# Weights of eight experts split into bf16 pairs in DRAM, and a quantised FFN whose work is shared out anew

## The chip, the cores and the metric

The kernel runs on one core of a Trainium2 chip. The metric is the device time of one execution in microseconds, and the lower it is the better. TensorE (PE) does matrix products and transposes, VectorE (DVE) and ScalarE (ACT) work on rows in SBUF and PSUM, GpSimd (POOL) does small work and issues gathers, scatters and casting DMAs, and SyncE (SP) issues the other DMAs.

## The reference, cut to what matters

The input x has 16 sequences of 128 tokens with 256 features; ctx_1024 has the same shape. Two layers follow one another, each an attention over the context and then a feed-forward network (FFN), with a layer norm before each and a residual sum after it.

```python
# layer 0: attention, 16 heads, softmax over the context's tokens of the same sequence
x = x + softmax(q @ k.T * scale) @ v @ Wout
# layer 0: FFN whose activations and weights are rounded to 8-bit levels
def _act_fake_quant(x, clip_factor):
    scale = jax.nn.sigmoid(clip_factor) * jnp.max(jnp.abs(x)) / QMAX
    return jnp.clip(_ste_round(x / scale), -QMAX - 1.0, QMAX) * scale
h = _act_fake_quant(jax.nn.silu(gate) * up, clip_down[0])     # 704 hidden columns
x = x + einsum(h, _weight_fake_quant(w_down))
# layer 1: mLSTM attention, 4 heads, gates from q, k and v of all tokens
# layer 1: mixture of 8 experts, each token goes to its 2 best
#   expert e: (silu(x @ w1[e]) * (x @ w3[e])) @ w2[e], w1, w3: 256 x 1024, w2: 1024 x 256
```

The maximum in the scale of an activation runs over all tokens and columns, so the FFN of layer 0 has two places where everything has to be finished before anything goes on.

## The kernel before, in words

All engines run their own program and meet at semaphores. The stages follow one another.

**Attention of layer 0.** A step per sequence b, 16 in all. PE writes scores of two groups of heads (`scores`), DVE subtracts the row maximum (`softmax_shift`), ACT takes the exponential and copies, PE transposes and multiplies. POOL's only part is `mask_k(b, p)`: two products of 256 columns that lay out k by heads, after ACT's copy `qk_evac` and before `scores(b)` of the next step. SP loads the context of sequence b + 2 when `t1_done` says that b's is used. In the last seven steps DVE also does a piece of the weight quantisation of layer 0's FFN (`rest`: `gate_up_maxima` to `early_norms`), long passes over weights in SBUF. At the very start POOL does four powers for the norms and then its first mask.

**Quantised FFN.** `activation_scale(0)`: DVE takes a maximum per partition, POOL one over partitions (`partition_all_reduce`). Then four groups g of 512 tokens with six column tiles t: PE does gate and up (`gate_up`), ACT the Silu (`silu`), DVE the product with the scales and a maximum over its result (`hidden`). After `activation_scale(1)` eight half groups n pass through the down product: DVE clips in two passes (`clip_above`, `clip_below`), ACT stores as bf16, PE multiplies, DVE scales the result, adds it to x and takes the statistics of the next norm (`add_down`). `x2_ready` counts the half groups that are added.

**Attention of layer 1.** PE does transposes, gates and scores of all sequences (`front_c`, `gates_and_scores`); SP loads the contexts for it. When `gates_read` says that all are done, SP stores the gates to DRAM and loads them back in another order (L419, L422), DVE scans them, SP stores and broadcasts the running maxima, POOL masks (`causal`), and then the sequences pass through the values and the router.

**Routing and experts.** DVE works out which token goes to which of 39 tiles of 128 rows (`NT` = 39); a tile belongs to one expert. A tile passes through `gate_up_half` twice, transposes and `down_d` on PE. Each product is made of three bf16 products: x and the weights are split into a high half and a low one (what the high half leaves). Tokens are gathered for a tile by POOL (`gather_rows`), results are added to `sum_dram` by a scattering DMA (`add_rows`). The weights of an expert come from the inputs as float32 when its first tile is near: SP loads w1, w3 and w2 under the condition `new > 0` into `stage` (`load_part`), ACT writes the high half (`weights_high`), DVE or POOL subtracts for the low one (`weights_low`), and PE waits for `part_low` at each tile. There are three places for experts in SBUF (`SLOTS`).

```python
            for t in range(2):
                for n in range(3):
                    load_part(n, t, t)
```

Of the kernel before, what the change touches and what calls it, by code (L numbers as in the profile page):

```python
# [8 lines left out]
def build(nc, x, ctx_in, wq, wkv, wout, clip_x, clip_down, w_gate, w_up, w_down, ig_k, ig_b, fg_k, fg_b, rms_scale,  # L9
# [10 lines left out]
    P = 128  # L20
# [17 lines left out]
    SLOT = 2 * 3 * PART  # L38
    H1 = ig_k.shape[1]
# [12 lines left out]
    with stack:  # L52
# [9 lines left out]
        def lay(region, *specs):  # L62
# [59 lines left out]
        tile_info = sb("tile_info", [P, 3, NT], I32)  # L122
# [9 lines left out]
        down_out = sb("down_out", [P, 2, D])  # L132
# [25 lines left out]

        hT, x1n, xq = lay(region2, (F32, IT, B * P), (F32, B, D), (BF16, KT, B * P))
# [18 lines left out]
         hT_hi, hT_lo, y_d, w_col, stage) = lay(  # L178
# [6 lines left out]
            (F32, 2, 3, PART))  # L185

        xrow, xn_r, xT_r, logits = lay(region2[:, 2 * SLOT // 2:], (F32, B, ROW), (F32, 2, D), (F32, 2, KT, P), (F32, B, E))
        expert_w = region2[:, :].bitcast(BF16)
        xrow_dram = nc.dram_tensor("xrow_dram", (B * P + P, ROW), F32, kind="Internal").ap()
# [72 lines left out]
        amax_all_ready = sem("amax_all_ready")  # L262
# [6 lines left out]
        amax_h_step = sem("amax_h_step")  # L269
        h_clipped = sem("h_clipped")  # L270
# [51 lines left out]
        tokens_placed = sem("tokens_placed")  # L322
# [8 lines left out]
        gap_ready = sem("gap_ready")  # L331
# [3 lines left out]
        places_done = sem("places_done")  # L335
# [3 lines left out]
        part_loaded = [[sem(f"part_loaded{i}_{p}") for p in range(2)] for i in range(3)]  # L339
        part_high = [sem(f"part_high{i}") for i in range(3)]  # L340
        part_low = [sem(f"part_low{i}") for i in range(3)]
# [30 lines left out]
        def _(sp):  # L372
# [9 lines left out]

            whole = (IT - 1) * P
# [18 lines left out]
            with sp.Fori(0, B // 2 - 1) as i:  # L402
                for p in range(2):

                    sp.wait_ge(t1_done, 2 * i + p + 1)
                    sp.dma_start(ctx_sb[:, p, :], ctx_in[2 * i + (p + 2), :, :]).then_inc(ctx_loaded[p], 16)
# [4 lines left out]
            with sp.Fori(0, B // 2 - 1) as i:  # L411
                for p in range(2):

                    sp.wait_ge(ct_done, 2 * i + p + 1)
                    sp.dma_start(ctx_c[:, p, :], ctx_in[2 * i + (p + 2), :, :]).then_inc(cctx_loaded[p], 16)
# [22 lines left out]
            with sp.Fori(0, B // 2 - 1) as i:  # L438
                for p in range(2):
                    sp.wait_ge(pvc_done, 2 * i + p + 1)  # L440
                    load_v(p, 2 * i + (p + 2))
# [9 lines left out]
            def load_part(n, t, p, inner=False):  # L451
# [3 lines left out]
                if inner or t >= 2:  # L455

                    sp.wait_ge(part_low[n], t - 1)
# [5 lines left out]
            for t in range(2):  # L463
                for n in range(3):
                    load_part(n, t, t)
# [1384 lines left out]
```

## Time and profile before

| | us |
|---|---|
| median of three runs (range) | 881.13 (877.24 to 881.49) |
| the profiled execution: its own time | 880.42 |
| the profiled execution: span from the first to the last instruction | 878.7 |
| PE, DVE, ACT, POOL busy in the span | 686.7, 545.8, 394.6, 248.4 |
| mean granted TensorE clock, of full speed | 0.867 |

Durations are taken from the profiled execution. Its time lies 1.7 us above its span, and 0.7 us under the median of the three runs. A mean over the span says little here, since the stages have different limits.

### The profile page before, as it was taken

How to read it: one execution, taken by the hardware profiler on the slowest of the kernel's cores; microseconds unless marked ns; L12 is line 12 of the kernel's file. 1: busy time of each engine (PE TensorE's matmuls, PEld its weight loads, DVE VectorE, ACT ScalarE, POOL GpSimd, SP SyncE). 2: the span in 40 equal slices, each digit the busy share in tenths (PEclk: the TensorE clock that was granted, in tenths of full speed). 3: DMA queues.
4: the chain of work that ended last, by engine and by line, in shares of the span. 5: the costliest groups of instructions: out<-in, count | busy, mean ns of one | idle time of the engine just before them, and what ended most of it. 6: DMA issues, size and time to landing. Idle time of an engine off the chain costs nothing.

```text
span 878.7 us, 19300 instructions
## 1 busy us (share of the span) xinstructions
PE 686.7 (78%) x4567; PEld 473.8 (54%) x4611; DVE 545.8 (62%) x1394; ACT 394.6 (45%) x811; POOL 248.4 (28%) x372
## 2 busy tenths in 40 slices
PE   3999999983745695277616989898989989889992
PEld 2778877761223473266513556565655655556661
DVE  5577789974989654398785464555455455564440
ACT  1466655544633254355314453535444545453330
POOL 3111111110000200644402353545344272653421
PEclk9799999985985598555556999999999999999996
DMA  8100000000000111511172433343251515431113
GB/s 256 31 13 14 15 12 12 0 1 0 1 0 0 31 54 30 211 31 30 41 248 66 127 73 87 104 125 73 37 160 24 167 30 166 127 72 24 30 25 108
DMA packets 45843, 58.41 MB, mean 66 GB/s; under 512 B 13496, under 2 KB 39416, under 8 KB 45272
## 3 DMA queue, kind: packets, MB, share of 16 engines
q1 hardware_dynamic: 38328, 47.79, 16.7%
q0 software_dynamic: 7488, 10.31, 7.4%
q8 instruction: 11, 0.18, 0.1%
q14 instruction: 16, 0.13, 0.0%
HBM read 145.90 MB, written 11.80 MB: 179 GB/s over the span
## 4 chain that ended last, share of the span: by engine, by line
PE 47%; DVE 20%; issue 15%; POOL 7%; DMA 3%; ACT 3%; DVEq 2%; ACTq 1%; POOLq 1%; SPq 0%
PE psum L962 16%; PE psum L984 7%; PE psum L698 3%; PE psum L975 3%; PE psum L682 3%; PE psum L705 2%; POOL region L638 2%; PE psum L862 2%; DVE region L1455 2%; PE psum L718 1%; PE psum L737 1%; DMA region<-xrow_dram,next_token 1%; PE psum L687 1%; PE psum L855 1%; POOL region L561 1%
## 5 line engine op out<-in xcount | busy, mean ns | idle before, releaser
L962 PE MATMUL psum<-region 128*128 x897 | 209.3, 381 | 18.9 <-issue 6.0
L962 PEld LDWEIGHTS psum<-region 128*128 128x128 bf16 x936 | 91.7, 98 | 117.8 <-issue 28.6
L984 PE MATMUL psum<-region 128*128 x936 | 113.9, 280 | 6.3 <-DVE region L1799 3.7
L984 PEld LDWEIGHTS psum<-region 128*128 128x128 bf16 x936 | 92.1, 100 | 23.1 <-issue 9.7
L1769 DVE TENSOR_TENSOR region<-psum,region 128x512 f32<-128x512 f32 x78 | 53.9, 691 | 72.8 <-ACT region L1209 63.5
L1209 ACT ACTIVATE region<-psum 128x512 f32<-128x512 f32 x78 | 46.5, 597 | 116.6 <-PE psum L962 108.2
L620 POOL DMA_INDIRECT sum_dram<-region,tok_idx x39 | 62.0, 1589 | 6.9 <-issue 6.6
L608 POOL TENSOR_TENSOR pause_p<-minus_half 128x1 f32<-128x1 f32 x37 | 7.1, 193 | 192.3 <-DVE next_token L1785 191.6
L1230 ACT ACTIVATE pause_a<-one_col 128x1 f32<-128x1 f32 x117 | 23.7, 202 | 83.9 <-issue 68.8
L1799 DVE TENSOR_TENSOR region<-psum,region 128x1024 bf16<-128x1024 f32 x39 | 47.7, 1222 | 19.1 <-ACT region L1217 19.1
L522 POOL TENSOR_TENSOR region<-region,pair_mask 128x256 f32<-128x256 f32 x32 | 18.9, 613 | 138.3 <-ACT region L1029 138.3
L609 POOL DMA_INDIRECT region<-xrow_dram,next_token x39 | 41.0, 1052 | 39.6 <-DVE next_token L1764 27.4
L1749 DVE MEMSET pause_d<- 128x1 f32 x80 | 4.7, 59 | 73.4 <-ACT pause_a L1233 39.1
L1304 DVE TENSOR_REDUCE region<-psum 128x8 f32<-128x1024 f32 x32 | 39.0, 1219 | 14.6 <-PE psum L698 14.5
L1217 ACT ACTIVATE region<-psum 128x1024 bf16<-128x1024 f32 x39 | 39.9, 1023 | 16.0 <-PE psum L975 15.0
L1232 ACT ACTIVATE region<-region 128x2048 f32 x24 | 45.8, 1909 | 0.0
L895 PE MATMUL psum<-region 128*128 128x96 f32 x128 | 32.0, 433 | 17.6 <-DVE region L1579 8.8
L1033 ACT ACTIVATE region<-region 128x1024 f32<-128x1024 f32 x32 | 33.8, 1057 | 25.8 <-DVE region L1306 25.8
L1751 DVE TENSOR_TENSOR region<-region 128x2048 f32 x17 | 39.0, 2294 | 2.6 <-issue 2.6
L698 PE MATMUL psum<-region 32*128 32x256 f32 x256 | 38.1, 417 | 3.0 <-POOL region L522 3.0
L975 PEld LDWEIGHTS psum<-ident,region 128*128 128x128 f32 x312 | 36.5, 141 | 7.4
L975 PE MATMUL psum<-ident,region 128*128 128x128 f32 x312 | 40.4, 273 | 0.0
(295 smaller groups left out, 1362.6 us busy)
## 6 DMA issues: line engine op xcount, KB each, us to landing
region<-in_L_ffn_w SPq DMA_DIRECT2D x117, 1024.0 KB
region<-in_ctx SPq DMA_DIRECT2D x48, 128.0 KB, 2.1
region<-neg_max_dram SPq DMA_DIRECT2D x4, 1024.0 KB, 7.6
xrow_dram<-region SPq DMA_DIRECT2D x1, 2080.0 KB, 7.8
x_sb<-in_x SPq DMA_DIRECT2D x4, 512.0 KB, 6.6
sum_dram<-x_sb SPq DMA_DIRECT2D x1, 2048.0 KB, 7.5
region<-in_L_ffn_w_down SPq DMA_DIRECT2D x1, 704.0 KB, 8.3
region<-in_L_ffn_w_gate SPq DMA_DIRECT2D x1, 640.0 KB, 8.9
```

Source lines behind the costliest of these rows:

```text
L609: pool.indirect_dma_start(xg[:, p, :], None, xrow_dram, bass.IndirectOffsetOnAxis(ap=next_token[:, p:p + 1], axis=0)).then_inc(xg_loaded[p ...
L620: pool.indirect_dma_start(sum_dram, bass.IndirectOffsetOnAxis(ap=tok_idx[:, p:p + 1], axis=0), y_d[:, p, :], None, compute_op=ALU.add).the ...
L698: last = mm(S_ps[s][:, 4 * r + 2 * m:4 * r + 2 * m + 2, :], qkT[rows, p, m, :], kbd[rows, p, m, :, :], start=True, stop=True)
L962: last = mm(psum[:, 2 * f + n, :], (xT_lo if xl else xT_hi)[:, p, k, :], weights_at(place, wl, n, k * F1 + f * FH, FH), start=(i == 0), st ...
L975: last = tr(bank(4, F1 // P, P, count=2)[:, f, :], h_d[:, p, f * P:(f + 1) * P], ident[:])
L984: last = mm(psum[:, 7, 0:D], (hT_lo if hl else hT_hi)[:, f, :], weights_at(place, wl, 2, f * D, D), start=(i == 0), stop=(i == 3 * (F1 // ...
L1209: act_fn(sil_d[:, f, :], psum[:, 2 * f, :], ACT.Silu).then_inc(sil_d_ready, 1)
L1217: act_fn(hT_hi, bank(4, F1 // P, P, count=2), ACT.Copy).then_inc(hT_high, 1)
L1232: act_fn(expert_w[:, bass.ds(place + n * PART, PART)], stage[:, p, n, :], ACT.Copy)
L1304: nc.vector.tensor_reduce(row_max[:, m, :], S_ps[m][:, :, :], AX.X, ALU.max).then_inc(max_ready, 1)
L1769: tt(h_d[:, p, f * FH:(f + 1) * FH], psum[:, 2 * f + 1, :], sil_d[:, f, :], ALU.mult).then_inc(h_d_ready, 1)
L1799: tt(hT_lo, bank(4, F1 // P, P, count=2), hT_hi, ALU.subtract).then_inc(hT_low, 1)
```

## The change: what it does

**Weights.** Each of the 24 parts (8 experts, w1, w3 and w2, 1 MB of float32 each) is split once and lies then in DRAM as `split_dram`, a high and a low half of bf16 side by side. For a part, SP loads the float32 weights, a casting DMA that POOL issues loads the same weights as bf16, POOL subtracts in four chunks of 512 columns, and SP stores the pair (1 MB). The first 16 parts go beside the 16 steps of layer 0's attention, with three buffers; the other 8 after `x2_ready`, beside the first half of layer 1's attention, with two buffers. The first two experts are loaded as pairs into their places during the values of layer 1's attention. In the expert stage SP loads the others in the order of their use, by registers from `expert_info`; PE waits for `expert_loaded` by a count that stands in `tile_info`; ACT, DVE and POOL convert nothing there. The context loads of layer 1's first half are issued by ACT.

**Quantised FFN.** The maximum over partitions comes from a product of a matrix of ones with a diagonal (`spread_peak`) in place of POOL's reduction. Of the column tiles with odd t, ACT also copies the scaled up product out of PSUM and POOL makes the product with the Silu; DVE keeps the maxima and the even tiles. In the down stage ACT scales and rounds, DVE clips once, POOL does the residual sum. A Silu of one column loads the activation table early. In `token_stats` the copy of the statistics becomes a maximum over one element.

```diff
+            def load_part(i):
+                view, width = weight_part(i)
+                if i >= 2:
+                    sp.wait_ge(part_split, i - 1)
+                sp.dma_start(whole_part(i)[0].rearrange("p (t f) -> p t f", f=width), view).then_inc(part_loaded[ring_of(i)], 16)
+            def store_part(i):
+                sp.wait_ge(part_split, i + 1)
+                sp.dma_start(split_dram[i // 3, i % 3, :, :], whole_part(i)[1]).then_inc(part_stored[ring_of(i)], 16)
+            load_part(0)
+            load_part(1)
...
+            for i in range(EARLY_PARTS):
+                if i + 2 < B:
+                    sp.wait_ge(t1_done, i + 1)
+                    sp.dma_start(ctx_sb[:, i % 2, :], ctx_in[i + 2, :, :]).then_inc(ctx_loaded[i % 2], 16)
+                store_part(i)
+                if i + 2 < EARLY_PARTS:
+                    load_part(i + 2)
 
             sp.wait_ge(x2_ready, B // 2)
             for b in range(2):
                 sp.dma_start(ctx_c[:, b, :], ctx_in[b, :, :]).then_inc(cctx_loaded[b], 16)
+            load_part(EARLY_PARTS)
+            load_part(EARLY_PARTS + 1)
+            for i in range(EARLY_PARTS, PARTS):
+                store_part(i)
+                if i + 2 < PARTS:
+                    sp.wait_ge(part_stored[ring_of(i)], 16 * uses(i))
+                    load_part(i + 2)
 
             sp.wait_ge(gates_read, B)
...
+            for b in range(B - 2):
+                sp.wait_ge(pvc_done, b + 1)
+                load_v(b % 2, b + 2)
+                if b < 6:
+                    sp.dma_start(expert_w[:, b // 3 * SLOT + b % 3 * 2 * PART:b // 3 * SLOT + (b % 3 + 1) * 2 * PART],
+                                 split_dram[b // 3, b % 3, :, :]).then_inc(first_experts, 16)
...
+            for j in range(E):
+                expert = sp.value_load(expert_info[0:1, j, 0:1], min_val=0, max_val=E - 1)
+                if j < 2:
+                    other = sp.value_load(expert_info[0:1, j, 2:3], min_val=0, max_val=1)
+                elif j >= 3:
+                    sp.wait_ge(dn_done, sp.value_load(expert_info[0:1, j - 3, 1:2], min_val=1, max_val=NT + 1))
+                if j >= 1:
+                    sp.wait_ge(expert_loaded, 48 * j)
                 for n in range(3):
...
+            def cast_part(i):
+                view, width = weight_part(i)
+                if i >= 3:
+                    last = i - 3 if i < EARLY_PARTS else i - 2
+                    if last >= (0 if i < EARLY_PARTS else EARLY_PARTS):
+                        pool.wait_ge(part_stored[ring_of(i)], 16 * uses(last))
+                nc.gpsimd.dma_start(whole_part(i)[1][:, 0:PART].rearrange("p (t f) -> p t f", f=width), view).then_inc(part_cast[ring_of(i)], 16)
+            def split_part(i):
+                whole, pair = whole_part(i)
+                pool.wait_ge(part_loaded[ring_of(i)], 16 * uses(i))
+                pool.wait_ge(part_cast[ring_of(i)], 16 * uses(i))
+                for c in range(0, PART, CHUNK):
+                    last = nc.gpsimd.tensor_tensor(pair[:, PART + c:PART + c + CHUNK], whole[:, c:c + CHUNK], pair[:, c:c + CHUNK], ALU.subtract)
+                last.then_inc(part_split, 1)
+            cast_part(0)
+            cast_part(1)
...
+            for b in range(B):
+                mask_k(b, b % 2)
+                split_part(b)
+                if b + 2 < EARLY_PARTS:
+                    cast_part(b + 2)
...
             pool.wait_ge(x2_ready, B // 2)
             nc.gpsimd.memset(q_only, 0.0).then_inc(q_preset, 1)
             nc.gpsimd.memset(v_c, 1.0).then_inc(q_preset, 1)
+            cast_part(EARLY_PARTS)
+            cast_part(EARLY_PARTS + 1)
+            for i in range(EARLY_PARTS, PARTS):
+                split_part(i)
+                if i + 2 < PARTS:
+                    cast_part(i + 2)
...
+            for t in range(1, IT, 2):
+                hidden_product(0, t)
...
+            def residual_add(n, q):
+                pool.wait_ge(down_read, n + 1)
...
+            def spread_peak(n):
+                pe.wait_ge(amax_ready, n + 1)
+                mm(psum[:, 6, 0:P], ones_sb[:], amax_diag[:], start=True, stop=True).then_inc(amax_spread, 1)
...
+                    if t % 2 == 1:
+                        act.wait_ge(up_done, IT * g + t + 1)
+                        act_fn(up_sb[:, t // 2, :], psum[:, 3, :], ACT.Copy, scale=gu_scale[:, IT + t:IT + t + 1]).then_inc(up_copied, 1)
...
+            def hidden_round(n):
+                part = hT[:, :, bass.ts(n, TB // 2)]
+                act_fn(part, part, ACT.Copy, bias=MAGIC, scale=act_inv[:, 1:2]).then_inc(h_rounded, 1)
...
-                nc.vector.tensor_copy(mv[:, b, :], mv1[:]).then_inc(chain, 1)
+                nc.vector.tensor_reduce(mv[:, b, :], mv1[:].unsqueeze(2), AX.X, ALU.max).then_inc(chain, 1)
...
-            def weights_low(n, t, p, inner=False):
...
+            link_d(nc.vector.tensor_scalar(e_used, etiles, 0.5, None, ALU.is_ge))
+            link_d(nc.vector.tensor_tensor_scan(e_rank, ones_sb[:, 0:E], e_used, -1.0, ALU.mult, ALU.add))
```

## Rows read from the trace of the kernel before

**Rows 1.** Busy us by stretch: PE, PEld, DVE, ACT, POOL; clock, DMA share, GB/s.

```profile
0.00:21.00 21.00, 5.95 (x24) 5.08 (x25) 12.37 (x55) 2.88 (x5) 8.15 (x24) 0.99 0.88 268
21.00:115.00 94.00, 93.28 (x864) 75.36 (x864) 66.72 (x125) 56.30 (x79) 10.77 (x19) 0.95 0.06 17
115.00:190.00 75.00, 68.09 (x636) 53.88 (x635) 65.99 (x125) 41.87 (x59) 9.37 (x13) 0.96 0.03 7
...
302.00:340.00 38.00, 38.00 (x240) 27.50 (x238) 19.14 (x44) 21.07 (x57) 0.00 (x0) 0.97 0.14 42
...
529.00:867.00 338.00, 308.70 (x1911) 196.65 (x1944) 170.03 (x441) 150.06 (x340) 145.67 (x204) 0.98 0.33 82
```

**Rows 2.** Chain that ended last, expert stage: start us, us, what.

```profile
472.20 3.80 PE psum L962 x11
...
538.60 2.76 PE psum L962 x12
...
547.80 2.76 PE psum L962 x12
...
848.68 2.59 PE psum L962 x12
```

**Rows 3.** Timeline of SP and POOL, first half of layer 1's attention.

```profile
293.54 0.81 SPq L410 DMA_DIRECT2D region<-in_ctx  x2
...
296.93 0.58 POOL L556 MEMSET region<- 128x584 f32 x1
...
340.21 0.65 SPq L419 DMA_DIRECT2D gates_dram<-region  x2
```

**Rows 4.** Timeline of the quantised FFN; brackets hold idle time and its end.

```profile
207.96 0.16 DVE L1431 TENSOR_TENSOR act_scale<-amax_all,clip 128x1 f32<-128x1 f32 x1 [4.25 <-POOL amax_all L545]
...
214.77 1.28 ACT L1105 ACT_TABLE_LOAD   x1 [1.50 <-PE psum L809]
...
232.38 0.74 DVE L1455 SCALAR_TENSOR_TENSOR region<-psum,gu_scale,sil 128x512 f32 x1
...
233.86 0.74 DVE L1455 SCALAR_TENSOR_TENSOR region<-psum,gu_scale,sil 128x512 f32 x1
...
276.64 0.68 DVE L1489 TENSOR_TENSOR down_out<-psum,down_scale 128x512 f32<-128x512 f32 x1
277.24 0.95 DVE L1480 TENSOR_SCALAR region<-region  x1
...
285.85 0.68 DVE L1489 TENSOR_TENSOR down_out<-psum,down_scale 128x512 f32<-128x512 f32 x1
```

**Rows 5.** Groups by form, 190 to 302 us: busy us, mean ns, idle before.

```profile
L1105 ACT ACTIVATE sil<-psum,gu_scale 128x512 f32<-128x512 f32 x24 | 16.4, 686 | 12.8 <-DVE region L1455 12.8
...
L1117 ACT ACTIVATE region<-region x8 | 11.9, 1483 | 25.2 <-DVE region L1480 25.2
...
L1459 DVE TENSOR_REDUCE amax_h<-region x18 | 12.4, 686 | 2.5
```

**Rows 6.** Groups by form of POOL over the whole span.

```profile
L609 POOL DMA_INDIRECT region<-xrow_dram,next_token x39 | 41.0, 1052 | 39.6 <-DVE next_token L1764 27.4 <-DVE region L1791 8.1 <-issue 1.7
L638 POOL TENSOR_TENSOR region<-region 128x2048 f32 x7 | 32.6, 4651 | 0.0
```

**Rows 7.** DMA issues: KB each, median us from issue to landing.

```profile
region<-in_ctx SPq DMA_DIRECT2D x48, 128.0 KB, 2.1
...
sum_dram<-x_sb SPq DMA_DIRECT2D x1, 2048.0 KB, 7.5
```

**Rows 8.** Timeline of layer 0's attention, PE, POOL and DVE.

```profile
21.17 2.08 PE L698 MATMUL psum<-region 32*128 32x256 f32 x8 [3.04 <-POOL region L522]
...
90.73 1.18 POOL L522 TENSOR_TENSOR region<-region,pair_mask 128x256 f32<-128x256 f32 x2 [8.74 <-ACT region L1029]
...
157.63 3.23 DVE L1372 TENSOR_SCALAR region<-region,w_inv 128x256 f32<-128x256 f32 x12
```

**Rows 9.** Layer 1's norm: count, ns min/median/max, first and last start.

```profile
L1528 DVE TENSOR_SCALAR region<-x_sb,mv,rstd x16: 397/408/1534, 296.1 to 334.7; 128x256 f32 x14, 128x256 f32<-128x256 f32 x2
```

More of the change, by code:

```diff
@@ L479, in _ @@
-            load_step(0, 0)
-            with sp.Fori(0, (NT - 5) // 2) as i:
-                load_step(2 * i + 1, 1, inner=True)
-                load_step(2 * i + 2, 0, inner=True)
-            for t in range(NT - 4, NT):
-                load_step(t, t % 2)
+            sp.wait_ge(info_ready, 2)
+            sp.wait_ge(rows_stored, 64)
+            sp.wait_ge(first_experts, 96)
+            for j in range(E):
[6 more added lines that the diff above has]
+                    sp.wait_ge(expert_loaded, 48 * j)
+                for n in range(3):
+                    at = j % 3 * SLOT + n * 2 * PART
+                    when = dict(cond=(other > 0)) if j < 2 else {}
+                    sp.dma_start(expert_w[:, at:at + 2 * PART],
+                                 split_dram.rearrange("e n p c -> p e n c")[:, bass.ds(expert, 1), n, :].rearrange("p e c -> p (e c)"),
+                                 **when).then_inc(expert_loaded, 16)
@@ L1093, in group_copy @@
                 act_fn(xq[:, :, g * TB:(g + 1) * TB], bank(6 + g % 2, KT, TB, dt=BF16), ACT.Copy).then_inc(xq_ready, 1)
+            act_fn(pause_a[:, 0:1], one_col[:], ACT.Silu)
             round_group(0)
@@ L1217, in h_high, with tile_step @@
                 act_fn(hT_hi, bank(4, F1 // P, P, count=2), ACT.Copy).then_inc(hT_high, 1)
[L1219 to L1235 removed]
+            def tile_step(t, p, inner=False):
                 silu_d(t, 0)
@@ L1510, in _, with down_scaled @@
-            for n in range(2):
-                clip_above(n)
-                clip_below(n)
-            with dve.Fori(0, G - 1) as g:
-                add_down(g)
+                dve.wait_ge(h_rounded, n)
+                nc.vector.tensor_scalar(part, part, MAGIC + QMAX, MAGIC - QMAX - 1.0, ALU.min, ALU.max).then_inc(h_clipped, 1)
+            def down_scaled(n, q, first=False):
+                dve.wait_ge(down_done, n + 1)
+                if not first:
+                    dve.wait_ge(x2_ready, n - 1)
+                nc.vector.tensor_tensor(down_out[q], bank(4 + q, 2, D), down_scale[:].unsqueeze(1).to_broadcast([P, 2, D]),
+                                        ALU.mult).then_inc(down_read, 1)
@@ new lines, in pair_stats @@
+            def pair_stats(n):
+                dve.wait_ge(x2_ready, n + 1)
+                nc.vector.memset(pause[:], 0.0)
+                for j in range(2):
+                    last = nc.vector.bn_stats(stats[:, j, :], x_sb[:, 2 * n + j, :])
+                last.then_inc(ln3_chain, 1)
+                dve.wait_ge(ln3_chain, 3 * n + 1)
+                nc.vector.memset(pause[:], 0.0)
+                for j in range(2):
+                    last = nc.vector.bn_aggr(mv2[:, j, :], stats[:, j, :])
+                last.then_inc(ln3_chain, 1)
+                dve.wait_ge(ln3_chain, 3 * n + 2)
+                nc.vector.tensor_copy(mv[:, bass.ds(2 * n, 2), :], mv2[:]).then_inc(ln3_chain, 1)
```

372 lines of the change are left out of this document (182 added, 190 removed).

## Prediction

> **What bounds the kernel now.** I read the stretches first [rows 1]: how busy each engine is in each stage, with the DMA columns at the end. In the attention of layer 0 (up to about 190 us) the reader is to see PE busy for 93.3 of 94 us in the first stretch, DVE for 66.0 of 75 in the second, and the DMA engines almost idle (share 0.06 and 0.03). In the first half of layer 1's attention PE is busy for 38.0 of 38.0 us. In the expert FFN PE is busy for 309 of 338 us. Then the chain of waits in the expert FFN [rows 2]: its first piece of a tile starts at 472.20, that of the last tile at 848.68, so 38 tiles take 9.91 us each, while a tile in which nothing is converted takes 547.80 - 538.60 = 9.20 us. The timeline of SP and POOL [rows 3] shows the third thing: SP issues the first context load of layer 1 at 293.54 and the store of the gates at 340.21. What follows in that layer waits for the store, and SP stands in line for it as any engine does. So there are four places to price, each by what sets its end.
>
> **1. Expert FFN: the conversions leave (-25 us).** Out go 39 x 3 loads under a condition, with a high and a low half made by ACT, DVE and POOL. PE is the bound in a quiet tile, so nothing goes below 9.20 us: 38 x (9.91 - 9.20) = -26.9. Against it stand 14 small DVE instructions that order the experts before the tokens are placed; they replace one subtraction of weights over 2,048 columns at that point, some +0.8 (0 to 3), and the first gathers beside a 3 MB expert load, +1. The loads themselves are early by one or two experts, each some five tiles (46 us), against 3.15 MB / 305 GB/s = 10.3 us (the rate is worked out in part 4). Registers per tile change from two loads to one of three values; I bound the quiet tile by 9.1 and 9.4 us (+-0.1 to 0.2 of 9.20), so the term lies between -29 and -17. I take -25.
>
> **2. Quantised FFN (-17 us).** The peak over partitions: DVE stands 4.25 us until POOL's reduction [rows 4]. In its place come a 128x128 product on DVE, one matmul and a 128-wide maximum, under 1 us together, and the four norms that DVE does meanwhile (some 1.4 us) become the cover that ends last: -3.5. The table load of 1.28 us for the first Silu [rows 4] moves ahead of its matmul: -1.3. The hidden loop is DVE's: one step each 233.86 - 232.38 = 1.48 us, 2.96 a pair [rows 4]. The new pair is one product and two maxima on DVE (0.74 + 0.69 + 0.69, overlapping to 2.0 to 2.1) beside two Silus and a scaled copy on ACT, 3 x 0.69 = 2.06 [rows 5]; POOL's product of 512 columns, by its rate in part 3, is 1.2. Taking 2.15 a pair, nine pairs give 9 x 0.81 = -7.3; in the first group ACT also rounds and copies, and three more copies on it cost +1. The second peak had waited little for POOL: +0.8. Down projection: one half group takes (285.85 - 276.64) / 2 = 4.60 us [rows 4], DVE's own work. One clip (0.95) and the residual sum (as long as the scaling, 0.68) leave it [rows 4], so 2.97 stay; ACT does two passes of 1.48 [rows 5], 2.97. So 3.0 to 3.1, with a slower start and the end held by a power of 2.3 us on POOL ahead of two of its additions: six steps by 1.5 less some 2 is -7. Sum -17; if POOL and DVE get in each other's way at each step, -12; without any of it, -21.
>
> **3. Layer 1's attention: eight parts in a row on SP's and POOL's way (+43 us).** This is the term that decides. After x2_ready POOL splits parts 16 to 23 with only two buffers. Its order is split i, wait for the store of i, issue the cast of i + 2, split i + 1. SP's is: wait for split i, store it, wait for that store, load i + 2. One part thus costs, one after the other: four chunks on POOL, by its subtraction of 128x2048 in 4.65 us [rows 6] 4.7; the store's landing, between 2.1 us for 128 KB and 7.5 us for 2,048 KB [rows 7], so 4.6 for 1 MB; the wake-ups and 1 MB of loads still moving ahead of it, 0.4; and the cast's issue, which no row shows: the nearest is the gather's 1.05 us for 128 rows [rows 6], a cast has 256, and 1,024 for every third part. I take 1.2, since most of such an issue looks fixed, and keep 0.8 and 3 as bounds. Sum 10.9 (9.5 to 12.3). Start: POOL is done with its two memsets at 297.51, 4.0 us after SP's 293.54 [rows 3]; two cast issues, 2.4, and the first cast's landing behind two loads and beside the second, 5: the first split begins at +11.5. Then 6 x 10.9 = 65.4 to split 22, 4.7 for it, some 2 until part 23 has landed, 4.7 for its split: +88 us. Only then does SP come to the gates, where it came at 340.21 - 293.54 = +46.7 [rows 3]: +41.5, and the gates' small store stands behind 1 MB on the same queue, +2. PE's 38 us of front work lie wholly under this, so that stage ends by SP, not by PE, and its context loads (now issued by ACT) and POOL's late memset cost nothing. If that cover were gone they would cost what they add; it isn't. Term +43, between +32 (9.5 a part, no queue) and +54.
>
> **4. Layer 0's attention: sixteen parts under PE (+8 us).** POOL idles 8.74 us in each 9.92 us step [rows 8]; 4.7 for a split and 1.2 for a cast fit. Three costs are left. At the start PE waits 3.04 us for POOL's first mask [rows 8], and two cast issues now stand ahead of it: +2.4. Next, the DMA engines: per step a load, a cast and a store of 1.05 MB and 0.13 MB of context. Opening traffic ran at 268 GB/s with share 0.88 [rows 1], 305 GB/s when full. If a cast counts by what it reads, a step's 3.28 MB need 10.7 us; by what it writes, 2.75 MB, 9.0. Against 9.92 that is 0 to 16 x 0.8 = 12 us; the later steps are longer, and I take +2. Last, DVE: in the later steps it is nearly the bound [rows 1] and does long passes over weights in SBUF, as the twelve that take 3.23 us [rows 8], while POOL subtracts. The norm of layer 1 takes 408 ns and 1,534 ns when a POOL memset runs [rows 9], so DVE can stand for a whole POOL instruction. Two chunks of 1.2 us can meet each of two such passes and one each of two more: up to 7; I take 4. The term is +8, from +2 to +24. The Trainium skill, "SBUF — State Buffer", section "Who interferes with whom", speaks against the change here: a DVE instruction in a two-port mode and a GpSimd instruction exclude each other for a whole instruction. By that rule, the trace agrees, and were every chunk in four steps to hit DVE, it would be 16 x 1.2 = 19 us rather than 4.
>
> **Sum.** -25 - 17 + 43 + 8 = +9. The profiled execution has a span of 878.7 us and a time of 880.4, so 889.4; the median of the three runs is 881.1, 0.7 above, so 890. A difference below 0.5% (4.4 us) can't be told from none here.
>
> **The rivals.** (a) *The late parts pass faster, and the kernel gains.* Everything else sums to -34, so the change breaks even at +34 for layer 1: 43 - 34 = 9 us over six parts, 1.5 each, at 9.4 us a part. At 8 us a part (a store landing in 3 us, the cast's issue at 0.8, the split at 4.1) it is 43 - 17 = 26, and the time 873. For it: the row of 2 MB has 1 KB rows and these stores have 8 KB. Against it: POOL's subtraction alone is half of the 9.4, and the two landings of rows 7 put 1 MB at 4.6. 20%. (b) *Attention of layer 0 does not hold the traffic*: casts that move at half rate, or chunks that meet DVE each time, as worked out in part 4: +15 more, 905. For it: the need of 9.0 to 10.7 us is at the step's length already; against it, stores may be late by a step without anyone waiting. 17%. (c) *Balance*: an expert tile that falls to 9.0 us and a split stage near 10 us a part: -8 and -5, about 880. 13%. The Trainium skill, "DMA: Bandwidth & Descriptors", section "Where 436 GB/s comes from", gives 358 GB/s from memory for one core; by that limit 3.28 MB need 9.2 us and (b) loses its first cause. No run here shows it; the opening row stays at 305.
>
> **How the numbers follow.** The forecast (my sum, 880 to 899) has 50%, (b) 17%, (a) 20%, (c) 13%. Of the forecast's cases a tenth falls under 885.5. Slower by over 0.5%: 0.43 + 0.17 = 0.60. Within: 0.07 + 0.10 = 0.17. Faster: 0.20 + 0.03 = 0.23. The range leaves out the far half of (a) and the far third of (b): 868 to 908.
>
> **What would show it.** Split parts on POOL from 16 to 23 about 11 us apart, and SP's store of the gates some 88 us after the first context load of layer 1; PE with a gap of some 40 us between the fronts and the values (wrong if the gap is under 30). Expert tiles at 9.2 us throughout, ACT and DVE without conversions. Pairs of 2.15 us and half groups of 3.0 us in the quantised FFN. In the first attention, steps still 9.9 us, with a DMA share of 0.9, and the later ones up to 1 us longer; if PE waits for POOL's masks in many steps, (b) is right. The prediction is wrong if POOL need not wait for its stores, or if direct casts cost POOL several us each.

## The result and the profile after

The changed kernel takes 927.9 us (median of four runs, 927.1 to 929.5), the kernel before 880.1 on the same chip (877.2 to 881.5): 1.055 of it, with a 95% interval of 1.052 to 1.058. It is slower by 48 us. The forecast was 890, with a range of 868 to 908, so the direction was right and the size was not. The profiled execution has a span of 925.5 us. The stretches of both kernels, cut where the same work ends, show where the 46.8 us between the spans are.

The stretches of the kernel before; the columns are those of [rows 1].

```profile
21.00:198.80 177.80, 168.63 (x1584) 134.77 (x1584) 138.58 (x270) 102.10 (x145) 20.14 (x32) 0.95 0.04 12
198.80:293.50 94.70, 50.72 (x220) 23.87 (x224) 76.52 (x163) 39.56 (x46) 4.06 (x4) 0.71 0.00 0
293.50:356.90 63.40, 42.74 (x258) 30.76 (x258) 26.60 (x69) 27.70 (x72) 2.48 (x4) 0.82 0.20 63
356.90:472.20 115.30, 57.45 (x261) 50.99 (x262) 92.03 (x320) 42.86 (x138) 46.93 (x77) 0.50 0.33 106
472.20:848.70 376.50, 347.34 (x2135) 218.97 (x2172) 193.89 (x507) 176.28 (x403) 161.41 (x227) 0.99 0.34 85
848.70:878.70 30.00, 13.84 (x87) 9.34 (x87) 5.80 (x12) 3.24 (x4) 5.24 (x6) 0.75 0.31 84
```

The same stretches of the changed kernel.

```profile
22.00:210.50 188.50, 170.54 (x1584) 135.56 (x1584) 144.45 (x270) 102.21 (x145) 106.38 (x111) 0.95 0.83 226
210.50:288.00 77.50, 42.76 (x224) 22.05 (x228) 57.51 (x141) 55.63 (x66) 32.71 (x22) 0.86 0.00 0
288.00:394.00 106.00, 53.62 (x258) 35.46 (x258) 48.86 (x68) 27.70 (x72) 44.57 (x43) 0.73 0.78 235
394.00:511.00 117.00, 57.49 (x260) 51.01 (x262) 90.21 (x329) 39.61 (x132) 45.62 (x77) 0.50 0.40 134
511.00:897.00 386.00, 340.79 (x2134) 219.26 (x2171) 146.02 (x339) 93.66 (x151) 108.98 (x148) 0.99 0.27 74
897.00:925.50 28.50, 12.53 (x87) 8.60 (x88) 5.20 (x9) 3.24 (x4) 5.04 (x5) 0.81 0.34 88
```

The reader is to see the length of each stretch, its second number. Layer 0's attention with its start ends 11.7 us later (198.8 to 210.5). The quantised FFN is 17.2 shorter, layer 1's attention up to POOL's masks 42.6 longer, the values and the routing 1.7 longer, the tail 1.5 shorter. The first four stand within 4 us of the forecast's terms (+8, -17, +43, and +1.8 for the ordering of the experts and the first gathers); the tail had no term. The 38 tiles of the expert stage were to be 26.9 us shorter and are 9.5 longer, at the same granted clock of 0.99, though DVE, ACT and POOL have lost 48, 83 and 52 us of work there. That one line is nearly the whole miss.

Two quiet tiles, PE's timeline: first the kernel before, then the changed one.

```profile
821.04 2.76 PE L962 MATMUL psum<-region 128*128 x12 [0.15 <-issue]
823.64 1.04 PE L975 MATMUL psum<-ident,region 128*128 128x128 f32 x8
824.73 2.54 PE L962 MATMUL psum<-region 128*128 x11
827.10 0.38 PE L969 MATMUL psum<-ident,region 128*128 128x128 f32 x2
827.32 2.78 PE L984 MATMUL psum<-region 128*128 x24
```

```profile
866.68 2.76 PE L1040 MATMUL psum<-region 128*128 x12 [1.08 <-issue]
...
872.96 2.78 PE L1061 MATMUL psum<-region 128*128 x24
876.83 2.76 PE L1040 MATMUL psum<-region 128*128 x12 [1.09 <-issue]
```

The products themselves take as long as before. What grew is the hole ahead of a tile's first product: 0.15 us became 1.08, and the tile went from the 9.20 of [rows 2] to 10.15 (10.50 where the loop turns). (The ends of products are modelled, so the lengths of tiles are the surer measure of a hole.) "issue" says that PE waited for nothing that the profile shows. The instructions on PE's sequencer that read tile_info show what it did there: the kernel before and then the changed one; count, ns min/median/max, first and last start.

```profile
L989 PEldq TENSOR_LOAD <-tile_info x78: 297/302/643, 470.1 to 856.6; - x78
```

```profile
L1066 PEldq TENSOR_LOAD <-tile_info x40: 766/770/954, 508.4 to 905.2; - x40
```

Before, two reads of one value per tile took 302 ns each, one at the tile's start and one ahead of `down_d`. The change makes it one read of three values, 770 ns, at the tile's start. A read is not over with its own time, as the same two tiles show: the sequencer's instructions of the read's line in the changed kernel (864 to 867 us) and then in the kernel before (819.5 to 821.5 us).

```profile
L1066 PEldq FUSED_REGOPS  x4: 46/148/154, 864.6 to 866.1; - x4
...
L1066 PEldq TENSOR_LOAD <-tile_info x1: 771/771/771, 864.7 to 864.7; - x1
```

```profile
L989 PEldq FUSED_REGOPS  x2: 46/98/151, 819.9 to 820.3; - x2
L989 PEldq TENSOR_LOAD <-tile_info x1: 299/299/299, 820.0 to 820.0; - x1
```

Behind the read come operations on the values (`FUSED_REGOPS`, about 0.29 us to the next one, a group for each value) and the waits of the tile, and only then the next weight load. From the read's start to that load it is 2.01 us in the changed kernel (864.66 to 866.67) and 1.06 before (819.97 to 821.04). In both the read starts some 0.93 us before the last queued product ends, so these products cover a part of it and the rest is the hole. The difference, 0.95 us, is what the tile grew by. Whether this read is the cause, or the wait against a register's value that stands behind it, or SP's expert loads, is what the experiments had to tell apart.

### The profile page after: what moved, and what is told of

Same layout as the page of the kernel before. It is cut to its first block, busy times and chain, and to the rows that moved or that the text cites. A ratio compares the mean times of both kernels' runs of the same rounds, so it can differ in the third digit from the quotient of the medians.

```text
span 925.5 us, 15569 instructions
## 1 busy us (share of the span) xinstructions
PE 683.7 (74%) x4571; PEld 477.0 (52%) x4615; DVE 504.6 (55%) x1208; ACT 324.9 (35%) x573; POOL 352.6 (38%) x428
## 4 chain that ended last, share of the span: by engine, by line
PE 47%; DVE 15%; issue 14%; DMA 10%; POOL 6%; SPq 4%; ACT 2%; DVEq 1%; POOLq 0%; ACTq 0%
PE psum L1040 20%; PE psum L1061 9%; DMA region<-split_dram 5%; POOL region L566 3%; PE psum L1053 3%; PE psum L765 3%; PE psum L749 2%; PE psum L772 2%; DMA region<-in_L_ffn_w 2%; PE psum L785 1%; PE psum L887 1%; SPq L440 1%; PE psum L804 1%; PE psum L754 1%; POOL region L643 1%
## 5 line engine op out<-in xcount | busy, mean ns | idle before, releaser
L1040 PE MATMUL psum<-region 128*128 x897 | 210.2, 383 | 47.2 <-issue 39.5
L566 POOL TENSOR_TENSOR region<-region 128x512 bf16<-128x512 f32 x96 | 111.3, 1187 | 14.8 <-DMA region<-in_L_ffn_w 14.7
L1061 PE MATMUL psum<-region 128*128 x936 | 108.6, 273 | 2.5 <-DVE region L1897 2.5
L702 POOL DMA_INDIRECT sum_dram<-region,tok_idx x39 | 61.9, 1587 | 10.6 <-issue 10.5
L1897 DVE TENSOR_TENSOR region<-psum,region 128x1024 bf16<-128x1024 f32 x39 | 47.7, 1224 | 21.9 <-ACT region L1322 21.9
L1384 DVE TENSOR_TENSOR region<-psum,region 128x1024 f32<-128x1024 f32 x32 | 39.2, 1224 | 1.1
L975 PEld LDWEIGHTS psum<-region 128*128 128x128 f32 x128 | 28.4, 328 | 20.4 <-issue 11.3
L749 PE MATMUL psum<-region 128*128 128x128 f32 x256 | 36.1, 302 | 2.8 <-DMA region<-in_L_xattn_Wout 2.8
```

Source lines behind the costliest of these rows:

```text
L566: last = nc.gpsimd.tensor_tensor(pair[:, PART + c:PART + c + CHUNK], whole[:, c:c + CHUNK], pair[:, c:c + CHUNK], ALU.subtract)
L702: pool.indirect_dma_start(sum_dram, bass.IndirectOffsetOnAxis(ap=tok_idx[:, p:p + 1], axis=0), y_d[:, p, :], None, compute_op=ALU.add).the ...
L749: last = mm(bank1[:, m, :], w, xcT[:, p, (m // KT) * KT + k, :], start=(k == 0), stop=(k == KT - 1))
L975: last = mm(psum[:, p, at:at + 96], decayed[:, p, h, :], v_c[:, p, at:at + 96], start=True, stop=True)
L1040: last = mm(psum[:, 2 * f + n, :], (xT_lo if xl else xT_hi)[:, p, k, :], weights_at(place, wl, n, k * F1 + f * FH, FH), start=(i == 0), st ...
L1061: last = mm(psum[:, 7, 0:D], (hT_lo if hl else hT_hi)[:, f, :], weights_at(place, wl, 2, f * D, D), start=(i == 0), stop=(i == 3 * (F1 // ...
```

## The experiments

Times are medians of four runs. The kernel before took 876.0, 880.5, 880.5 and 875.6 us in the four sessions, so differences between kernels of different sessions are taken from their ratios to it, times 880.

**e1: the read moved ahead of queued products.**

```diff
                 place, place_before, loads = info_of(t)
+                if inner or t >= 2:
+                    down_d(t - 2, place_before, inner)
                 pe.wait_ge(expert_loaded, loads)
...
-                if inner or t >= 1:
-                    down_d(t - 1, place_before, inner)
```

> The changed kernel, but the three register values of a tile are read ahead of the down products that precede it (column 1 of the table holds the place of tile t-2, and TensorE's loop is rotated), so that the read passes beside queued matmuls. The matmuls, their order and the wait on the experts' loads stay. Theory A (the three-value read of 0.77 us, exposed at each tile's start, is what tiles of 10.15 us pay for): tiles of 9.2 to 9.4 us, 38 periods of about 355 us instead of 386, the kernel at 893 to 902 us. Theory B (the wait against a register's value, or the experts' transfers, holds TensorE): tiles stay at 10.1 us and the kernel at 926 to 929.

Measured: 895.7 us, 1.023 (1.020 to 1.025) of before, 28 us less than the changed kernel by the ratios. Most tiles take 8.89 us, less than theory A's 9.2 to 9.4, with the register wait and SP's loads still in place. Theory A holds and B falls.

**e2: the kernel before with the three-value read.**

```diff
-                place = place_of(t)
+                place, place_before, _ = info_of(t)
...
-                    down_d(t - 1, place_of(t - 1), inner)
+                    down_d(t - 1, place_before, inner)
```

> The kernel before with one piece of the change: TensorE reads three values at the start of a tile from a table of four columns, and none ahead of the down products; weights are still converted in the tile loop and no wait against a register is added. Theory A: each tile pays 0.77 instead of 0.30 us at its start and saves nothing that was exposed, +0.45 us on 38 tiles, +12 to +20 us (892 to 900). Theory B: the read costs nothing by itself, 880 within 3 us.

The table is laid out for this by tile, so the other engines read it at other places; their reads take 0.26 to 0.29 us (0.27 to 0.31 before).

Measured: 899.9 us, 1.028 (1.025 to 1.031), so +24 by the ratio; the expected +12 to +20 was too little. Alone, without any wait added, the read costs about half of what the whole change cost, and it does to a quiet tile what the change did: 10.25 us (9.20 before, 10.15 in the changed kernel). The 38 tiles take 396.5 us in place of 376.5. PE's idle time before `gate_up_half` reads 38.3 us of "issue" over the stage, against 37.3 in e6, which has the changed kernel's tiles.

**e3: no late parts.** Parts 16 to 23 are not split, and experts 5 to 7 use expert 4's weights.

```diff
-    PARTS = 3 * E
+    PARTS = 16
...
+            nc.vector.tensor_scalar_min(expert_info[:, :, 0], order, 4.0)
```

> The changed kernel without the splitting of parts 16 to 23 in layer 1's attention; experts 5 to 7 take expert 4's weights in their place, so that the experts' loads and products are as many as before. If these eight parts stand whole in the way of the gates' store, the stretch to the masks returns from 106 to about 63 us and the kernel falls by 43 us, to 883 to 887. If part of the 43 us is given back later, or if something else in this stretch takes time too, it falls by less, say 25 to 35 us (893 to 903).

Measured: 886.5 us, 1.012 (1.010 to 1.015): 38 us less by the ratio, 41 in microseconds. SP's first context load to POOL's masks is 352.00 - 287.26 = 64.7 us in its trace (106.2 in the changed kernel, 63.3 before). The spans of the two profiled executions differ by 925.5 - 883.5 = 42.0 us and the stage by 41.5, so in the traces nothing of it is given back later; that the ratio gives 38 is left open.

**e4: the kernel before with the quantised FFN alone.** Its edit is the FFN part of the change, shown in the diff ahead of the prediction.

> The kernel before with the rebalanced quantised FFN alone (peak spread by a matmul, odd hidden chunks through ScalarE and GpSimd, the rounding on ScalarE, the residual adds on GpSimd, the Silu table loaded ahead). If the 17 us that the stage gave in the changed kernel are the FFN's own, the kernel falls to 861 to 865. If they came from elsewhere (a warmer clock or other cover), it falls by under 12 us, to 868 or more.

Measured: 860.2 us, 0.982 (0.979 to 0.986), 15.8 us under the kernel before in its session. The gain is the FFN's own.

**e6: SP's small loads issued later.**

```diff
-            for n, w in enumerate((ig_b, fg_b)):
-                for b in range(B):
-                    sp.dma_start(gbias[b * H1:(b + 1) * H1, n:n + 1], w.unsqueeze(1)).then_inc(gk_loaded, 16)
             for i in range(EARLY_PARTS):
...
+            for n, w in enumerate((ig_b, fg_b)):
+                for b in range(B):
+                    sp.dma_start(gbias[b * H1:(b + 1) * H1, n:n + 1], w.unsqueeze(1)).then_inc(gk_loaded, 16)
             sp.wait_ge(x2_ready, B // 2)
```

> The changed kernel with one move in SP's queue: the 32 loads of the gates' biases, the gate weights, the scale and the two stores of empty rows are issued after the 16 early parts instead of ahead of the loop. Theory A: context 2 waited for these issues and for nothing else, step 1's 3.9 us wait for region from ctx_in goes, and layer 0's attention ends 5 to 8 us earlier (920 to 923 us). Theory B: context 2 is late because the transfers are full (share 0.97), the wait stays within 1 us, and the kernel stays at 926 to 929.

Measured: 922.4 us, 1.048 (1.045 to 1.050), 6 us less. SP's and PE's timelines of the changed kernel show the cause.

```profile
24.14 6.10 SPq L440 DMA_DIRECT2D gbias<-in_L_xattn_igate_bias  x16
30.28 5.81 SPq L440 DMA_DIRECT2D gbias<-in_L_xattn_fgate_bias  x16
...
38.41 0.47 SPq L450 DMA_DIRECT2D region<-in_ctx  x1
```

```profile
22.76 2.08 PE L765 MATMUL psum<-region 32*128 32x256 f32 x8 [4.88 <-POOL region L578]
...
40.78 0.49 PE L736 MATMUL psum<-ident,region 128*128 128x128 f32 x2 [3.92 <-DMA region<-in_ctx]
```

SP issues context 2 at 38.41, behind 32 bias loads of 0.37 us each; PE waits 3.92 us for it until 40.78. The kernel before has the same bias loads in front and issues it at 31.72, just in time: the two loads of parts and slower issues had put SP 5.1 us behind by its first bias load. After the wait the granted clock is at its lower level (0.50, 1.2 GHz, from 41 to 46 us; 1.00 in the kernel before):

```profile
41.00:46.00 5.00, 5.00 (x23) 3.84 (x22) 1.18 (x3) 1.54 (x2) 0.73 (x1) 0.50 0.98 282
```

How long the stage took shows in DVE's 16 sums onto x, one per sequence (count, ns, first and last start): the kernel before, the changed one, e6, and e7, which follows.

```profile
L1320 DVE TENSOR_TENSOR x_sb<-x_sb,psum x16: 420/420/423, 43.2 to 198.8; 128x256 f32 x8, 128x256 f32<-128x256 f32 x8
L1398 DVE TENSOR_TENSOR x_sb<-x_sb,psum x16: 420/422/423, 51.0 to 210.5; 128x256 f32 x8, 128x256 f32<-128x256 f32 x8
L1399 DVE TENSOR_TENSOR x_sb<-x_sb,psum x16: 420/422/422, 46.6 to 206.3; 128x256 f32 x8, 128x256 f32<-128x256 f32 x8
L1404 DVE TENSOR_TENSOR x_sb<-x_sb,psum x16: 420/422/422, 52.7 to 208.3; 128x256 f32 x8, 128x256 f32<-128x256 f32 x8
```

In e6 the wait is gone. From the first scores to the first sum it is 22.0 us before (from 21.17), 28.3 in the changed kernel (from 22.76) and 22.0 in e6 (from 24.62): wait and low clock together cost 6.3 us, all of it removed. The last sum is only 4.2 us earlier, less than theory A's 5 to 8, because this execution's first scores came 1.9 us later. Such a later start also stands in traces whose code is the changed kernel's up to there (24.31 in e1, 22.83 in e8) and was not explained.

**e7: the early parts without the subtraction.** Parts 0 to 15 keep every transfer, and their low halves are zero.

```diff
+                if i < EARLY_PARTS:
+                    if i < 3:
+                        nc.gpsimd.memset(pair[:, PART:2 * PART], 0.0).then_inc(part_split, 1)
+                    else:
+                        nc.gpsimd.memset(pair[:, PART:PART + 2], 0.0).then_inc(part_split, 1)
+                    return
```

> The changed kernel with every transfer of the early parts kept, but without the subtraction on GpSimd in parts 0 to 15 (the low halves are set to zero once, so the first 16 parts' products use the high halves alone). Theory A (DVE and GpSimd hold each other up): the last four steps of layer 0's attention, which were 3.9 us longer than before, go back, layer 0 ends 4 us or more earlier, and DVE's mean times there are those of before; 918 to 924 us. Theory B (the transfers, or their issue, made layer 0's attention longer): its end moves by less than 1.5 us, 926 to 929.

Measured: 923.5 us, 1.049 (1.045 to 1.052), in theory A's range, though the interval touches that of the changed kernel (1.052 to 1.058). By the rows of the sums, first to last takes 155.6 us before, 159.4 in the changed kernel and 155.5 in e7: the 3.8 us go back in full, with every transfer kept, and theory A holds. The last sum is only 2.2 us earlier (theory A had 4 or more) because this execution's first scores came 1.5 us later. DVE's weight passes in the late steps, grouped by form, in the changed kernel and then in e7:

```profile
L1384 DVE TENSOR_TENSOR region<-psum,region 128x1024 f32<-128x1024 f32 x9 | 11.0, 1224 | 0.3
...
L1450 DVE TENSOR_SCALAR region<-region,w_inv 128x256 f32<-128x256 f32 x12 | 5.0, 490 | 0.0
...
L1454 DVE TENSOR_SCALAR region<-region 128x3072 f32<-128x3072 f32 x1 | 2.6, 2600 | 0.0
```

```profile
L1390 DVE TENSOR_TENSOR region<-psum,region 128x1024 f32<-128x1024 f32 x9 | 11.0, 1225 | 0.3
...
L1456 DVE TENSOR_SCALAR region<-region,w_inv 128x256 f32<-128x256 f32 x12 | 3.2, 350 | 0.0
L1460 DVE TENSOR_SCALAR region<-region 128x3072 f32<-128x3072 f32 x1 | 1.8, 1755 | 0.0
```

Passes from SBUF to SBUF were longer beside POOL's subtraction (490 against 350 ns, 2,600 against 1,755), DVE's own subtraction that reads PSUM was not (1,224 and 1,225). By the Trainium skill, "SBUF — State Buffer", section "Who interferes with whom", a DVE instruction in a two-port mode and a GpSimd instruction exclude each other for a whole instruction. The trace agrees in that some of DVE's passes took longer by 3 us together; which of them run in such a mode no row shows.

**e5: late parts in the tiles.** From here on the question is which version beats both kernels. e5 is e1 and e6 together, with parts 16 to 23 split in the first eleven expert tiles.

```diff
-        late_ring = region2[:, B * P + KT * 2 * P:B * P + KT * 2 * P + 2 * 2 * PART].rearrange("p (r n) -> p r n", r=2)
+        late_ring = region1[:, 24480 - 3 * 2 * PART:24480].rearrange("p (r n) -> p r n", r=3)
...
+            for t in range(13):
+                step_d(t, t % 2)
+                for i in casts.get(t, []):
+                    cast_part(i)
+                late_chunks(t)
```

> The read-ahead version (895.7 us) with parts 16 to 23 converted in the expert stage (ring of three buffers at the end of region1, three chunks of a split on GpSimd in each of the first eleven tiles, all of SP's transfers of these parts ahead of its fourth expert) and with the small loads moved behind layer 0's attention. If the 43 us before the masks, the 7 us of late context loads and the exposed read are separate costs that are each removed once, it takes 896 - 43 - 7 + 0 to 8 = 846 to 854 us. If the splits hold up the gathers and adds in the first eleven tiles, or DVE beside them, these tiles go back to 9.5 to 10.5 us and the kernel takes 855 to 870.

Measured: 862.8 us, 0.981 (0.979 to 0.984). The masks come at 346.89, 47 us earlier than in the changed kernel. That is in the second case's range, not the first's: among tiles of 8.89 us stand some of 10.5 to 15.3, both beside the late parts and at each expert's loads. e5, e9 and e11 hold for a routing in which every expert gets at least one token, since the late parts are only awaited ahead of the fourth expert's load.

**e8 and e9: the traffic spread.** In e8 (on e1) the second and third load of an expert wait one tile longer; e9 is e5 with that and with slower pacing.

```diff
                 for n in range(3):
+                    if j >= 3 and n == 1:
+                        sp.wait_ge(dn_done, sp.value_load(expert_info[0:1, j - 3, 3:4], min_val=1, max_val=NT + 1))
```

> The read-ahead version (895.7 us), with one change: of the three 1 MB loads of an expert, the first is issued when the expert three places back is done, as now, and the other two one tile later (a fourth column of the experts' table). Theory A: the tiles of 10.5 us among those of 8.89 are tiles whose gathered rows land late behind a 3 MB burst (transfers at a share of 1.0), so that TensorE's queue runs empty and the register read behind it is bare again; with the burst cut in two the stalls at the five bursts of experts 3 to 7 shrink or go, 4 to 8 us less (888 to 892). Theory B: each of the two bursts now does it, the kernel stays at 895 or gains a stall each, up to 903.

> The version with the late parts in the tiles (862.8 us), with two of these parts split on GpSimd during the routing, ahead of the first gather, then two chunks a tile in place of three over the first twelve tiles, and the experts' loads spread as in e8. If GpSimd's and the transfers' load in the first eleven tiles cost the 13 us that these tiles lie over 8.89 us, about half of it goes and the experts' bursts give 3 to 5 us: 849 to 856 us. If DVE's routing is held up by the two splits, the first tile starts 3 to 6 us later and the kernel stays at 858 to 864.

Measured: e8 891.0 us, 1.013 (1.010 to 1.016); e9 867.1, 0.985 (0.981 to 0.988). The time of e8 is in theory A's range (888 to 892). But in the traces 29 tiles take 266.6 us where e1's take 269.7, so the edit gave some 3 us there, less than theory A's 4 to 8, and at each burst a tile of 10.2 to 11.1 us stays. For e9 neither forecast holds (849 to 856, 858 to 864). Its two splits during the routing delay SP's first expert load from 34.3 to 38.8 us after the store of the sums, and from the first down product on 36 tiles gain only 1.9 us on e5. Pacing is not the remedy.

**e10: the kernel before with the FFN and its own reads ahead of the down products,** by e1's edit.

> The kernel before with the rebalanced quantised FFN (860.2 us) and, in the tiles, the two single-value reads put ahead of the down products with TensorE's loop rotated. Theory A (a read at the head of a tile is bare even when it is of one value): quiet tiles fall from 9.20 to 8.9 us, and the tiles that convert weights by less, as other engines bound them: 848 to 854 us. Theory B (0.30 us lies beside the queued matmuls and costs nothing): 858 to 862 us.

Measured: 861.2 us, 0.980 (0.976 to 0.984), the same as e4 within the intervals and in theory B's range. But theory B's reason is wrong: quiet tiles fall to 8.9 us, so even a read of one value had been bare, and others grow, two of them to 14 and 15. e1's trace shows why; the first row is PE's weight load, the others are its products.

```profile
572.48 0.30 PEld L1047 LDWEIGHTS psum<-ident,region 128*128 128x128 f32 x2 [0.18 <-DMA region<-xrow_dram,next_token]
572.63 0.38 PE L1047 MATMUL psum<-ident,region 128*128 128x128 f32 x2
...
574.52 1.72 PE L1061 MATMUL psum<-region 128*128 x14 [1.51 <-issue]
```

The transposes of the next tile's rows stand ahead of the read. When the rows are late by as little as 0.18 us PE's queue is empty, and the read with what follows it is bare again, as a hole of 1.51 us. Behind the longest holes the clock falls as well: in e5, after 1.94 and 1.61 us of idle time, the granted clock is 0.50 from 511 to 516 us and the 24 down products take 5.30 us in place of 2.8, which makes the tile of 15.3.

**e11 and e12: the read in front of the rows.** e11 is e5 with e8's loads, e12 is e10, each with this edit; the order of PE's products stays that of the kernel before.

```diff
                 place, place_before, loads = info_of(t)
                 if inner or t >= 2:
+                    x_transposes(t, p, loads_x, inner)
                     down_d(t - 2, place_before, inner)
...
-                if inner or 0 < t < NT - 1:
-                    x_transposes(t + 1, 1 - p, loads_next, inner)
```

> The version with the late parts in the tiles (862.8 us, 0.981 of the kernel before), with the experts' loads spread as in e8 and TensorE's register read put one step further ahead: behind the second half of the gate and up products and in front of the transposes of the gathered rows, which may have to wait for them. The order of TensorE's products stays. Theory A (the stalls of 1.5 to 2 us, on one tile in four, are the read made bare because it stands behind a wait for late rows): a late row costs its own wait alone, ten stalls of 1.5 us go and the kernel takes 842 to 850 us (0.957 to 0.966). Theory B (the stall belongs to the late rows or to the full transfers, not to the read): 858 to 863 us.

> The kernel before with the rebalanced FFN and both single-value reads in front of the transposes of the gathered rows. The reads behind the rows gave 861.2 us (0.980): quiet tiles of 8.9 us, but tiles with late rows of 11 to 13. Theory A: with the reads in front, late rows cost no more than they do in the kernel before, quiet tiles stay at 8.9, and the kernel takes 846 to 853 us (0.962 to 0.969). Theory B: 858 to 862 us.

Measured: e11 844.2 us, 0.967 (0.961 to 0.972); e12 851.1, 0.971 (0.967 to 0.975). In microseconds both are where theory A had them; by the ratio each is 0.1 or 0.2% above its range. PE's timeline of e11:

```profile
488.70 2.78 PE L1085 MATMUL psum<-region 128*128 x24
...
497.59 2.78 PE L1085 MATMUL psum<-region 128*128 x24
...
506.94 0.44 PE L1071 MATMUL psum<-ident,region 128*128 128x128 f32 x2 [0.52 <-DMA region<-xrow_dram,next_token]
507.21 2.78 PE L1085 MATMUL psum<-region 128*128 x24
```

Tiles take 8.89 us while the late parts are being split beside them, and a late row costs little more than its own wait: 0.52 us of it make a tile of 9.62, and the longest, 2.62 us, one of 11.79. e11 has two edits on e5; e12 on e10 has the read's place alone and shows what it gives, 10 us. e11 beats both kernels, by 3.3% and (0.967 / 1.055) 8.4%.

## Why the prediction was wrong, point by point

**1. Expert FFN: the step that failed.** It said "Registers per tile change from two loads to one of three values; I bound the quiet tile by 9.1 and 9.4 us". The quiet tile measured 10.15, so the tiles gave 386.0 - 376.5 = +9.5 in place of -26.9, and 38 x 0.95 = 36 us are that whole miss, out of 38 for the kernel. The ordering and the gathers gave +1.7 (1.8 taken). The error was to count reads instead of asking where each stood and what comes behind it. The read ahead of `down_d` had cost nothing; the one at the tile's start had been bare by 9.20 - 8.89 = 0.31 us already (e12's quiet tile). So "nothing goes below 9.20 us" was wrong too: PE's own work is 8.89. All three values were put at the tile's start: 10.15 - 8.89 = 1.26 us bare, since the read is 0.47 us longer and two more groups of register operations stand behind it. That the conversions leave PE's path was right: with the read covered, quiet tiles take 8.89 us (e1, e11). No rival held this mechanism, and the range left it out.

**2. Quantised FFN: -17, measured -17.2,** and -15.8 by itself in e4. Pairs take 2.0 us (predicted 2.15), as two products in DVE's timeline of the changed kernel show, and half groups 2.8 (3.0). Both are better than the forecast, by some 2.5 us together, so the sum was in part right by luck. In the down stage DVE waits 3.62 us for the first product (1.6 before) and stands 2.99 us before its last statistics, where the forecast had taken some 2 us for both; that would account for it, and was not tried.

```profile
241.63 0.74 DVE L1533 SCALAR_TENSOR_TENSOR region<-psum,gu_scale,sil 128x512 f32 x1
...
243.63 0.75 DVE L1533 SCALAR_TENSOR_TENSOR region<-psum,gu_scale,sil 128x512 f32 x1
```

**3. Layer 1's attention: +43, measured +42.9** from the first context load to the masks. SP's and POOL's timelines of the changed kernel:

```profile
287.96 0.82 SPq L457 DMA_DIRECT2D region<-in_ctx  x2
...
374.99 0.83 SPq L469 DMA_DIRECT2D gates_dram<-region  x2
```

```profile
301.19 4.49 POOL L566 TENSOR_TENSOR region<-region 128x512 bf16<-128x512 f32 x4 [7.62 <-DMA region<-in_L_ffn_w]
310.85 0.72 POOL L559 DMA_DIRECT2D region<-in_L_ffn_w  x1 [5.17 <-DMA split_dram<-region]
311.60 4.47 POOL L566 TENSOR_TENSOR region<-region 128x512 bf16<-128x512 f32 x4
```

The gates' store comes at 374.99 - 287.96 = +87.0 us (predicted +88). A part takes 10.4 us (10.9): 4.5 for the split, 5.2 until the store has landed, 0.7 for the cast's issue, where 1.2 had been taken. The first split begins at +13.2 (11.5), so two small errors cancel in part. e3 confirms the term. Rival (a) falls: it needed 9.4.

**4. Layer 0's attention: +8, measured +11.7,** a term mis-sized. The start gave 1.6 (2.4 taken), no more than the unexplained difference between starts that e6 shows. The transfers gave no lasting delay (+2 taken): the early steps take 9.93 us as before, at a DMA share of 0.83. But the context that stood behind SP's small loads gave 6.3 us in steps 1 and 2, with the low clock behind it (e6), which was not in the sum: SP's queue was looked at for layer 1 and not here. The late steps gave 3.8 (4 taken), all of it POOL's subtraction (e7), and DVE's passes beside it are 3.0 of that. POOL's split took 4.5 us in most steps and 6.0 in the last two. Rival (b), +15 over the forecast from this stage, did not come.

The stretches sum to 9.5 - 17.2 + 42.6 + 11.7 + 1.7 - 1.5 = 46.8, the difference of the spans. "Slower" with 0.60 was right, but nearly all of the excess over the forecast's +9 came from a term that had been booked as a gain. Two small sums of the forecast don't close: rival (c) comes to 890 - 13 = 877, not 880, and the part of the forecast under 885.5 is booked as 0.07 of 0.50, a seventh and not a tenth. Neither moves the range.

## What to carry to other kernels

A register read on a sequencer costs what its place makes it cost. Price it with the register operations and waits that follow it, and set against that the products still queued when it starts: it costs nothing where they last longer, the difference where they don't, and all of it behind a wait for a transfer that comes late. So read in front of such a wait, not behind it. In a queue that issues transfers, many tiny ones ahead of one that is waited for can cost more than the megabytes beside them. A stage on whose path transfers and waits stand one after the other can be summed from single rows with good precision; what broke the forecast was a small thing, bounded by a guess, times 38.

## What the runs showed of the hardware

- A read of one int32 into a PE register took 0.30 us and of three 0.77; the hole in PE's products that they leave in a quiet tile was 0.31 and 1.26 us. The longer read leaves more than its own time because each value has its group of register operations behind it, 0.29 us apart; the read starts 0.93 us before the last queued product ends.
- PE's idle time of 3.92 us in layer 0's attention was followed by a granted clock of 0.50 for some 5 us, and so were the 3.55 us of two holes close together in e5's tiles.
- POOL's issue of a casting DMA for 1 MB took 0.72 us in layer 1's attention and 0.82 on the mean in layer 0's, with transfers at a share of 0.83 in that stretch.
- The Trainium skill, "DMA: Bandwidth & Descriptors", section "Where 436 GB/s comes from", gives some 358 GB/s as the limit from memory for one core. The measurement differs: in e1, which runs on one core, while an expert's three loads of 1 MB ran, the last column (all queues, the gathers among them) reads 407 and 391 GB/s.

```profile
570.00:572.00 2.00, 2.00 (x12) 0.93 (x11) 1.40 (x2) 1.02 (x1) 0.00 (x0) 1.00 0.99 407
572.00:574.00 2.00, 1.01 (x6) 0.46 (x4) 0.99 (x2) 0.87 (x2) 0.00 (x0) 1.00 1.04 391
```
